# Shifted-window attention block with MLP and divisive normalisation: the mean is taken out of weight columns, variances are put together on GpSimd, and two steps of TensorE's order are moved

## The reference

```python
def _ln(x, w, b):
    m = x.mean(-1, keepdims=True)
    v = ((x - m) ** 2).mean(-1, keepdims=True)
    return (x - m) / jnp.sqrt(v + EPS) * w + b
...
y = _ln(x, norm1_w, norm1_b)                       # over 96 channels of a token
y = jnp.roll(y, (-ss, -ss), axis=(1, 2))           # then cut into windows of 64 tokens
qkv = y @ qkv_w.T + qkv_b                          # q scaled by hd ** -0.5
attn = softmax(q @ k.T + mask)                     # per window and head
out = (attn @ v) @ proj_w.T + proj_b               # rolled back
x = shortcut + out
h1 = gelu(_ln(x, norm2_w, norm2_b) @ mlp_w1.T + mlp_b1)
x = x + (h1 @ mlp_w2.T + mlp_b2)
...
denom_sq = einsum('nchw,ic->nihw', x * x, gamma_eff) + beta_eff
x = x * rsqrt(denom_sq)
```

## Time and profile before

| | |
|---|---|
| time, median of 3 runs | 1769.26 us (1768.22 to 1774.46) |
| profiled execution, span | 1766.9 us; its own time is not listed beside the span |
| TensorE busy | 1720.2 us (97%) |
| VectorE busy | 1629.6 us (92%) |
| ScalarE busy | 1527.5 us (86%) |
| GpSimd busy | 1356.5 us (77%) |
| granted TensorE clock, mean | 0.993 |

### The profile page before, as it was taken

How to read it: one execution, slowest core, us unless ns; L and a number is a source line. 1 busy time by engine, 2 the same in 40 slices (tenths; PEclk the granted TensorE clock), 3 DMA queues, 4 the chain that set the end, 5 groups by cost and what they waited for, 6 DMA issues and landing times.

```text
span 1766.9 us, 81406 instructions
## 1 busy us (share of the span) xinstructions
PE 1720.2 (97%) x32612; PEld 1252.8 (71%) x32612; DVE 1629.6 (92%) x4508; ACT 1527.5 (86%) x2832; POOL 1356.5 (77%) x1532
## 2 busy tenths in 40 slices
PE   4999999999999999999999999999999999999996
PEld 2677777777777777777777777777777777777763
DVE  5899999999999999999999999999999999999983
ACT  2798998988898988988898888998888898998986
POOL 3478878878878878878778877888878878878862
PEclk9999999999999999999999999999999999999997
DMA  2122122122122122122122122122122122122111
GB/s 58 27 46 52 37 54 52 37 54 53 37 53 52 36 54 52 38 53 52 36 55 52 36 55 50 37 56 52 35 56 49 37 56 51 37 55 52 28 32 27
DMA packets 215154, 81.35 MB, mean 46 GB/s; under 512 B 116118, under 2 KB 214780, under 8 KB 214780
## 3 DMA queue, kind: packets, MB, share of 16 engines
q1 hardware_dynamic: 214218, 76.04, 19.7%
q10 hardware_dynamic: 562, 0.11, 0.0%
HBM read 25.75 MB, written 25.17 MB: 29 GB/s over the span
## 4 chain that ended last, share of the span: by engine, by line
PE 96%; DVE 1%; issue 1%; ACT 1%; DMA 0%; SPq 0%; POOL 0%; POOLq 0%; DVEq 0%
PE mm_bank L999 49%; PE score_banks L1058 8%; PE score_banks L947 7%; PE mm_bank L1105 6%; PE mm_bank L1032 5%; PE pv_bank L1081 5%; PE turn_banks L939 5%; PE turn_banks L953 3%; PE mm_bank L1094 3%; PE mm_bank L1091 3%; PE score_banks L1066 1%; PE mm_bank L1134 0%; DMA x_ext<-in_x 0%; DVE stats L767 0%; SPq L378 0%
## 5 line engine op out<-in xcount | busy, mean ns | idle before, releaser
L457 POOL TENSOR_TENSOR hidden_lo<-hidden,hidden_hi 128x512 fp32r<-128x512 f32 x378 | 480.9, 1286 | 0.0
L618 ACT ACTIVATE hidden<-mm_bank 128x512 f32<-128x512 f32 x381 | 227.8, 598 | 124.1 <-PE mm_bank L999 111.8
L539 ACT ACT_TABLE_LOAD x253 | 324.6, 1283 | 4.5
L452 POOL TENSOR_SCALAR y_hi<-y 96x512 fp32r<-96x512 f32 x128 | 108.1, 845 | 206.8 <-ACT y L563 206.8
L812 DVE TENSOR_REDUCE row_max<-score_banks 128x8 f32<-128x512 f32 x384 | 250.8, 681 | 10.8 <-PE score_banks L1066 8.1
L820 DVE TENSOR_TENSOR shifted<-score_banks,row_max 128x512 f32<-128x512 f32 x384 | 250.7, 680 | 0.0
L469 POOL TENSOR_TENSOR x_sq<-x 96x512 f32<-96x512 f32 x126 | 130.8, 1038 | 152.2 <-DVE x L846 152.2
L585 ACT ACTIVATE probs<-shifted 128x512 f32<-128x512 f32 x384 | 236.2, 627 | 10.6 <-DVE shifted L820 3.4
L452 POOL TENSOR_SCALAR hidden_hi<-hidden 128x512 fp32r<-128x512 f32 x378 | 229.8, 619 | 1.3 <-ACT hidden L618 1.3
L597 ACT ACTIVATE probs_t<-score_banks 128x512 f32<-128x512 f32 x384 | 215.1, 602 | 0.0
L767 DVE BATCH_NORM_STATS2 stats<-turn_banks 128x6 f32<-128x96 f32 x1024 | 191.1, 248 | 17.1 <-PE turn_banks L939 17.1
(11 more groups left out here) (132 smaller groups left out, 4489.2 us busy)
## 6 DMA issues: line engine op xcount, KB each, us to landing
x_ext<-in_x SPq DMA_DIRECT2D x128, 192.0 KB, 2.9
k_block<-k SPq DMA_DIRECT2D x768, 32.0 KB
out<-o_ext SPq DMA_DIRECT2D x128, 192.0 KB, 2.6
w_raw<-in_w_t SPq DMA_DIRECT2D x1, 144.0 KB
w<-in_w_t SPq DMA_DIRECT2D x1, 144.0 KB
qkv_raw<-in_qkv_t ACTq DMA_DIRECT2D x1, 108.0 KB
ident_sb<-in_ident SPq DMA_DIRECT2D x1, 64.0 KB, 2.2
q_quadrants<-in_qmask SPq DMA_DIRECT2D x3, 1.0 KB
```

The lines of the kernel that those rows point to most:

```text
L452: nc.gpsimd.tensor_scalar(hi, whole, 1.0, 1.0, ALU.mult, ALU.mult).then_inc(hi_ready, 1)
L457: nc.gpsimd.tensor_tensor(lo, whole, hi, ALU.subtract).then_inc(is_split, 1)
L539: nc.scalar.preload_act_table_set(name)
L618: nc.scalar.activation(hidden_of(A)[:, n, :], up_bank(A, n), ACT.Gelu).then_inc(gelu_ready, 1)
```

## The change

Four things are done.

1. The mean is no longer subtracted from the tokens. Instead each folded weight matrix (query, key, value, first MLP) has the mean over its 96 input rows taken out of every column once, at the start: TensorE multiplies with a matrix of ones (`qkv_column_sums`, `w1_column_sums`), and VectorE adds -1/96 of that. `bn_aggr` and the centring in place are gone.
2. GpSimd makes 96 times the variance from what `bn_stats` leaves (count, mean, count times variance for even and for odd elements), for both norms at once, in `variances`; ScalarE divides by 96 in the logarithm's scale. `rstd_pair` waits for `spread_ready`.
3. `project_q` moves from behind `project_v` to behind `denominators`, in TensorE's order and in `MM_ITEMS`; `q_copy` on ScalarE moves forward, `log_sums` back, and the log of the denominators ahead of `rstd_pair`.
4. `mlp_up` 0 moves ahead of `turn_in` of norm 1, so that both `turn_in` stand side by side. On VectorE `split_y2` moves ahead of `outputs`, and on GpSimd `rest_of_y1` ahead of `square`.

```diff
@@ MM_ITEMS
             ("den", DIVIDE, log_den_made, 1, 1),
+            ("q", QK, q_ready, 1, 1),
             ("sum", ATTEND - 1, log_sum_made, 1, 1),
             ("v", ATTEND, v_ready, 1, 1),
-            ("q", QK, q_ready, 1, 1),
@@ GpSimd
+            def variances(H):
+                lns = [ln for ln, offset in ((0, TURN_IN), (1, PROJECT)) if has(H + offset)]
+                if not lns:
+                    return
+                for ln in lns:
+                    wait_alone(pool, stats_made[ln], H + (TURN_IN, PROJECT)[ln] + 1)
+                slot, count = (H + 1) % 2, spread_count(H)
+                lns = slice(lns[0], lns[-1] + 1)
+                made = stats[:, slot, lns, :, :]
+                nc.gpsimd.tensor_tensor(mean_gap[:, lns, :], made[:, :, :, 1], made[:, :, :, 4], ALU.subtract)\
+                    .then_inc(gap_made, 1)
+                nc.gpsimd.tensor_tensor(within[:, lns, :], made[:, :, :, 2], made[:, :, :, 5], ALU.add)\
+                    .then_inc(gap_made, 1)
+                wait_alone(pool, gap_made, 2 * count)
+                nc.gpsimd.tensor_tensor(gap_sq[:, lns, :], mean_gap[:, lns, :], mean_gap[:, lns, :], ALU.mult)\
+                    .then_inc(gap_squared, 1)
+                wait_alone(pool, gap_squared, count)
+                nc.gpsimd.tensor_scalar(gap_part[:, lns, :], gap_sq[:, lns, :], DIM / 4, None, ALU.mult)\
+                    .then_inc(gap_scaled, 1)
+                wait_alone(pool, gap_scaled, count)
+                if H - 1 >= -TURN_OUT:
+                    wait_alone(pool, log_var_made, H - 1 + TURN_OUT + 1)
+                nc.gpsimd.tensor_tensor(spread[:, slot, lns, :], within[:, lns, :], gap_part[:, lns, :], ALU.add)\
+                    .then_inc(spread_ready, 1)
+                wait_alone(pool, spread_ready, count)
...
                 run(round_y1, TURN_OUT)
+                run(rest_of_y1, TURN_OUT)
                 run(square, SETTLE)
                 run(round_squares, SETTLE)
-                run(rest_of_y1, TURN_OUT)
                 run(rest_of_squares, SETTLE)
+                variances(H)
@@ ScalarE
-                for ln in lns:
-                    act.wait_ge(moments_ready[ln], H + (TURN_OUT, MLP)[ln] + 1)
+                act.wait_ge(spread_ready, spread_count(H - 1))
...
-                nc.scalar.activation(log_var[:, slot, lns, :], moments[:, slot, lns, :, 1], ACT.Ln,
-                                     bias=eps_col[:, :]).then_inc(log_var_made, 1)
+                nc.scalar.activation(log_var[:, slot, lns, :], spread[:, slot, lns, :], ACT.Ln,
+                                     bias=eps_col[:, :], scale=1.0 / DIM).then_inc(log_var_made, 1)
...
                 run(k_copy, QK)
+                run(log_denominators, DIVIDE)
                 if H >= -TURN_OUT:
                     rstd_pair(H)
-                run(log_denominators, DIVIDE)
                 run(softmax_exp, ATTEND, 0)
-                run(log_sums, ATTEND - 1)
+                run(q_copy, QK)
                 run(softmax_exp, ATTEND, 1)
                 run(softmax_exp, ATTEND, 2)
+                run(log_sums, ATTEND - 1)
                 run(inverse_sums, PROJECT)
-                run(q_copy, QK)
@@ VectorE, statistics
-                for n, c in enumerate(chunks_of(a)):
-                    made = nc.vector.bn_stats(stats[ln][:, c, :],
+                H = norm_round(A, ln) - 1
+                wait(dve, spread_ready, spread_count(H - 2))
+                for n in range(CHUNKS):
+                    made = nc.vector.bn_stats(stats[:, (H + 1) % 2, ln, n, :],
                                               turn_banks[:, ln, n * DIM:(n + 1) * DIM])
                 made.then_inc(stats_made[ln], 1)
-                wait_alone(dve, stats_made[ln], A + 1)
-                slot = norm_round(A, ln) % 2
-                for n, c in enumerate(chunks_of(a)):
-                    made = nc.vector.bn_aggr(moments[:, slot, ln, n, :], stats[ln][:, c, :])
-                made.then_inc(moments_ready[ln], 1)
-                dve.wait_ge(moments_ready[ln], A + 1)
-                nc.vector.tensor_tensor(turned(ln), turned(ln),
-                                        moments[:, slot, ln, :, 0:1].broadcast_to([128, CHUNKS, DIM]),
-                                        ALU.subtract).then_inc(centred[ln], 1)
@@ VectorE, order of a round, and the folding of the weights
+                run(split_y2, MLP)
                 run(outputs, DIVIDE)
-                run(split_y2, MLP)
...
+                dve.wait_ge(column_sums, 1)
+                for n, folded in enumerate((wq[0:DIM, :], wk[0:DIM, :],
+                                            wv[0:DIM, :, :, :].rearrange("c e p d -> c (e p d)"))):
+                    nc.vector.scalar_tensor_tensor(folded, score_banks[0:DIM, 1, n * DIM:(n + 1) * DIM],
+                                                   -1.0 / DIM, folded, ALU.mult, ALU.add).then_inc(weights_folded, 1)
@@ TensorE, order of a round
                 run(denominators, DIVIDE)
+                run(project_q, QK)
                 run(sum_probs, ATTEND - 1)
                 run(times_v, ATTEND - 1)
                 run(project_v, ATTEND)
-                run(project_q, QK)
                 turn_run(H)
                 for n in range(HID_CHUNKS):
                     run(mlp_down, SETTLE, n)
                 run(project, PROJECT)
+                run(mlp_up, MLP, 0)
                 run(turn_in, TURN_IN, 0)
                 if H == -TURN_IN:
                     qkv_bias_product()
+                    qkv_column_sums()
                 if H == -TURN_IN + 1:
                     w1_bias_product()
-                run(mlp_up, MLP, 0)
+                    w1_column_sums()
                 run(turn_in, PROJECT, 1)
```

48 lines of the change are left out of this document (38 added, 10 removed).

## The result

The changed kernel takes 1849.88 us, median of four runs (1847.43 to 1850.69), against 1769.26 before: 1.0447 times as long, 95% interval 1.0428 to 1.0465, or about 80 us. The forecast was 1798, with a range up to 1817. The sign is right and the size is not. The profiled execution took 1847.43 us and spans 1845.6.

What follows compares the result with a forecast made beforehand. TensorE, busy 97% of the span, was taken as the bound. 0.28 lost less 0.05 gained is 0.23 us a round, over 126 rounds 29.0, plus 0.3 once: 1769.26 to 1798.6, stated as 1798, range 1759 to 1817.

Steps and rivals of the forecast that it cites:

- VectorE's relief at nothing: On VectorE, dropping aggregation and centring saves 2.3 us a round, but gains nothing, since TensorE doesn't wait for it.
- GpSimd hidden, but barely: GpSimd's five small operations take 1.7 us with the last wait; its loop of 13.0 us fits a round of 13.3.
- Rival C: GpSimd becomes the bound, its loop longer than a round from about 2.1 us of small operations: 1886 us; chance 0.08.
- Queries beside the keys, 0.05 gained: On TensorE, q behind the denominators enters one rounded group less: gain between 0 and 0.18 us a round, taken as 0.05.
- V to the turn: On TensorE, the change of tile shape from v to the turn, in no row, was taken to cost about 0.10 us.
- the regrouping itself gains: On TensorE, queries beside the keys mean one group of rounded matmuls is entered less, which saves time.
- The new order around `mlp_up` 0, 0.28 lost: TensorE waits for x3 in front of `mlp_up` 0: 0.23 us a round, 0.34 with `outputs` blocked; middle 0.28.
- The block of `outputs` by y_hi: GpSimd's y_hi, starting first, may hold up VectorE's `outputs` by 0.1 us, making the stall 0.34 instead of 0.23.
- Sum: 0.28 lost less 0.05 gained is 0.23 us a round, over 126 rounds 29.0 us; with 0.3 once, 29.3 us.

Runs made afterwards that it cites:

- b6: Kernel before with the mean taken out of the weights and the centring gone, `bn_aggr` kept on VectorE, every order as before: 1764.0 us, ratio 0.9957.
- b2: Kernel before with one edit, `mlp_up` 0 directly behind `project` and ahead of `turn_in`: 1848.0 us, ratio 1.0441.
- c1: Changed kernel with the variances on VectorE again (`bn_aggr`) and without GpSimd's five small operations: 1870.5 us, ratio 1.0563.
- b4: Changed kernel less TensorE's two moves (`project_q`, `mlp_up` 0), with `rest_of_y1` early and `split_y2` ahead of `outputs` kept: 1798.9 us, ratio 1.0150.
- v2: b6 with the query products behind the denominators, written into the bank of `times_v`, which then waits for `q_copy`: 1811.4 us, ratio 1.0219.
- a3: Changed kernel with the query products back between values and turn, on TensorE, in bank order and on ScalarE: 1821.8 us, ratio 1.0290.
- b3: Kernel before with only the query products moved beside the keys, with the bank order and ScalarE's order of the changed kernel: 1804.2 us, ratio 1.0171.
- a2: Changed kernel with `outputs` back in front of `split_y2` on VectorE: 1836.7 us, ratio 1.0373.
- d2: Changed kernel with 5 to 23 small unused matmuls in front of `mlp_up` 0 of six rounds, 114 in all: 1857.5 us, ratio 1.0490.

## Why the prediction was wrong, step by step

**VectorE's relief at nothing: right in the order it was argued for.** b6 shows it for one microsecond a round: the rounds are 0.02 shorter. But it was argued from TensorE's unbroken time before the change, and the new order needs this relief: without it the loop through x3 and `turn_in` is 13.85 (b2).

**GpSimd hidden, but barely: true of the changed kernel, and barely.** c1 without this work has the same regular rounds. Without the cover of TensorE's new stalls GpSimd is the bound (b4). The prediction had 1.7 us for the small operations and a loop of 13.0; they hold it for 2.05, with 0.39 behind the last one, and y_lo is stretched by 0.2 more. Rival C was to decide from 2.1, but against the mean round of 13.17, with which the rival was priced, the same sum gives 1.9; it was nearer than its 0.08.

**Queries beside the keys, 0.05 gained: wrong, and this step failed most.** In the regular rounds it costs 0.06: q starts 0.15 after `k_copy`, not 0.06, and that alone is 0.09. V to the turn was sized well. That the regrouping itself gains was right: where q need not wait for `k_copy`, it brings 0.22 (v2). The wait, 0.24 of the 0.47 from den to q, takes that and a little more. What was missing altogether is that q's three long matmuls split the run of short ones. With q gone, 164 short matmuls follow one another, TensorE runs through a block of 256 instructions in 2.0 to 2.7 us, and the next block comes late: 18 us here (a3), 26 us in the kernel before (b3). In the kernel before, the same stops take 3 us in all. No term of the sum stood for them, since the sum took one round times 126.

**The new order around `mlp_up` 0, 0.28 lost: the mechanism was right, the size was 0.39.** x3 ends 4.67 us behind the turn's first transpose (499.89 to 504.56) where the prediction's times give 4.62 (511.62 to 516.24), and `split_y2` ahead of `outputs` counted, 0.10 a round (a2). The missing 0.10 is again the start of TensorE after the release, 0.15 for the 0.05 assumed; the prediction's own rows had 0.14 there. b2 has the same 0.15. Whether it hangs on the rounded operands, on the tile or on the weights to be loaded first is open. The block of `outputs` by y_hi didn't come; VectorE reached `outputs` as y_hi ended.

**Sum.** Per round 0.23 + 0.11 (`mlp_up` 0) + 0.11 (q costing 0.06 instead of gaining 0.05) = 0.45, of 0.48 measured: 57 to 61 us. Late instructions add 18. The sum over parts is not one of independent terms: with the variances on GpSimd, the mean costs 80 us in the old orders and 30 in its own, and `mlp_up` 0 alone costs 79. It is the longest of TensorE's, VectorE's and GpSimd's loops that sets the round. The parts lie almost at the same length, 13.4 to 13.9, whichever of them is taken.

A stop is long or short by how soon the packet of instructions starts behind the boundary before and how long it takes; at 1062.62 it started 0.52 late and took 1.52, and the gap was 1.24, at 1004.56 it was 0.20 and 1.08, and the gap was 0.46. Still open: what sets these two, since some packets start up to 3 us behind the boundary even in long rounds.

## What to carry to other kernels

Where an engine issues long runs of short instructions, count them: a stop of TensorE between two equal matmuls, put down to "issue" and recurring at a fixed count, was here the instruction stream, which the packets of kind "instruction" confirm. Three long matmuls inside the run hid it, so their place was worth more than the price between groups that their move was to save. Before moving a consumer forward, write down the whole loop that its new wait closes, over every engine in it, and not only the stall at the place; a relief that is worth nothing today may be what keeps that loop open. And when the bound is one engine by a few tenths, price each restart behind a wait from a row of the same kind of instruction.

## What the runs showed of the hardware

- TensorE's instructions come in blocks of 256: 261 packets of 16 KB for 66,911 instructions. No boundary was passed sooner than 1.16 us after the end of its packet, and the packet took 0.9 to 1.6 us (changed kernel; 1.8 at most in the others). Where TensorE ran through a block in less than 2.7 us, it nearly always stopped at the end, for 0.2 to 1.3 us, in v2 for up to 1.8. 124 unused instructions in front of everything moved those stops by dozens of rounds and changed the time by 12.7 us.
- A GpSimd instruction that is under way holds up a VectorE one with two inputs in SBUF for the rest of its length: 0.68 became 1.64 and 1.74 us, and both times it ended 0.54 to 0.55 us after GpSimd's.
- A wait of 1.65 us was followed by about a round at the lower clock level two times of four (c1), and 46 matmuls of one column over 1.5 us were three times of three (d2); the mean granted clock of such a round was 0.77 and 0.81. Stops of 1.2 us in the changed kernel were not (1.00).
- A rounded matmul of 512 columns started 0.15 us after the end of the operation that it waited for, a plain one of 384 columns 0.05 to 0.06 (the sum behind `k_copy`), and a plain one of 64 columns 0.26 (`times_v` behind `q_copy`, v2).
- A GpSimd operation on 128x8 elements took 0.20 to 0.23 us, and each wait for its own result 0.18 to 0.39 more.
